# Moving pieces and turns ahead of the weighing in the slots that begin a new block of columns

## What is computed

```
x = x + layernorm(attention(layernorm(x)))
x = x + layernorm(ffn(layernorm(x)))

scores  = q k^T, causal mask, / sqrt(512)
weights = softmax(scores)
attention = (weights v) @ Wo
ffn = relu(h + coef * sin(theta + 0.1 h)) @ W2 + b2,   h = x @ W1 + b1
```

## Time and profile before

| | |
|---|---|
| median of 3 runs | 3336.05 us (3333.89 to 3338.84) |
| the profiled execution | 3334.82 us, its span 3332.8 us |
| busy: TensorE, VectorE, ScalarE, GpSimd | 3150.9, 2327.5, 2063.6, 1280.2 us |
| share of the span | 95%, 70%, 62%, 38% |
| mean granted clock of TensorE | 0.991 |
| attention, roughly | 587 to 1932 us of the span |

### The profile page before, as it was taken

How to read it: one execution, slowest core, us unless ns; L and a number is a source line. 1 busy time by engine, 2 the same in 40 slices (tenths; PEclk the granted TensorE clock), 3 DMA queues, 4 the chain that set the end, 5 groups by cost and what they waited for, 6 DMA issues and landing times. The chain is left out here.

```text
span 3332.8 us, 77773 instructions
## 1 busy us (share of the span) xinstructions
PE 3150.9 (95%) x30020; PEld 1830.6 (55%) x30020; DVE 2327.5 (70%) x4793; ACT 2063.6 (62%) x2451; POOL 1280.2 (38%) x574
## 2 busy tenths in 40 slices
PE   6999998899998999999999879999999999999998
PEld 3444444676766676667676634444444444444443
DVE  5665555688887888888888666666666666666665
ACT  2323332998988898989898935555555555555553
POOL 1000000898989898989898910000000000000000
PEclk9999999999999999999999989999999999999999
DMA  4564753123222222222222230000000000000000
GB/s 140 190 206 139 259 189 112 53 60 85 73 85 74 77 79 78 77 75 78 79 75 81 89 127 6 21 26 26 25 25 25 25 25 25 25 25 25 26 26 26
DMA packets 194113, 246.65 MB, mean 74 GB/s; under 512 B 16960, under 2 KB 135936, under 8 KB 191616
## 3 DMA queue, kind: packets, MB, share of 16 engines
q1 hardware_dynamic: 193792, 242.25, 23.2%
HBM read 148.87 MB, written 92.80 MB: 73 GB/s over the span
## 5 line engine op out<-in xcount | busy, mean ns | idle before, releaser
L1426 POOL TENSOR_TENSOR a_prob_lo<-a_prob,a_prob_hi 128x2048 f16<-128x2048 f32 (+2 forms) x448 | 1191.7, 2694 | 148.9 <-ACT a_prob_hi L1285 147.8
L313 DVE TENSOR_REDUCE u_mx<-a_pw 128x4 f32<-128x512 f32 (+1 forms) x1178 | 728.4, 656 | 192.2 <-PE a_pw L299 127.5
L1275 ACT ACTIVATE a_prob<-a_pst,a_lift,w_exp_scale 128x1024 f32<-128x1024 f32 (+1 forms) x640 | 707.4, 1123 | 131.7 <-PE a_pst L1212 90.7
L1285 ACT ACTIVATE a_prob_hi<-a_prob 128x2048 f16<-128x2048 f32 (+2 forms) x448 | 584.0, 1304 | 0.0
L1731 ACT ACTIVATE f_hidden_work<-f_ph,w_turn,w_fold 128x512 f32<-128x512 f32 x256 | 199.4, 779 | 586.5 <-PE f_ph L1777 586.0
L1777 PE MATMUL f_ph<-f_xT,f_w 128*128 128x512 f16 x2304 | 528.6, 379 | 0.0
L1798 PE MATMUL f_py<-f_w,f_act 128*128 128x512 f16 x2280 | 523.1, 379 | 0.1
L1212 PE MATMUL a_pst<-u_qp,u_kp 98*128 98x256 f16 (+1 forms) x2560 | 464.3, 263 | 36.8 <-ACT a_prob L1275 16.6
L228 POOL TENSOR_TENSOR s_ve<-s_mv,s_eps 128x4 f32<-128x4 f32 x31 | 8.9, 286 | 1273.0 <-DVE s_mv L214 1273.0
L1239 PEld LDWEIGHTS a_acc<-u_vt,a_prob_hi 128*128 128x128 f16 x9216 | 422.6, 96 | 128.7 <-POOL a_prob_lo L1426 38.2
L1239 PE MATMUL a_acc<-u_vt,a_prob_hi 128*128 128x33 f16 x9216 | 448.6, 178 | 43.2 <-POOL a_prob_lo L1426 34.4
(11 more groups left out here) (187 smaller groups left out, 4089.4 us busy)
## 6 DMA issues: line engine op xcount, KB each, us to landing
qk_parts<-q_stage SPq DMA_DIRECT2D x128, 256.0 KB, 3.3
u_qp<-qk_parts SPq DMA_DIRECT2D x192, 128.0 KB, 2.6
u_kp<-qk_parts SPq DMA_DIRECT2D x192, 128.0 KB, 2.7
v_parts<-q_vstage SPq DMA_DIRECT2D x16, 1056.0 KB, 5.3
u_vt<-v_parts SPq DMA_DIRECT2D x32, 528.0 KB, 4.3
q_x<-in_L_attn_h_dram SPq DMA_DIRECT2D x16, 1024.0 KB, 10.2
q_raw<-in_L_ffn_W_dram SPq DMA_DIRECT2D x16, 1024.0 KB, 8.1
u_xr<-in_L_attn_h_dram SPq DMA_DIRECT2D x64, 256.0 KB, 3.0
```

The source lines that it names most:

```text
L313: dve.tensor_reduce(out, src[:, 0:n * len(heads)].rearrange("p (h n) -> p h n", n=n), AX_X, ALU.max).then_inc(units.released, 1)
L1275: act.activation(prob[:, k % PR, :, off:QC], pst[:, k % 2, :, off:QC], ACT.Exp, scale=exp_scale, bias=lift[:, :]).then_inc(exp_done, 1)
L1285: act.activation(prob_hi[:, first % HR:first % HR + steps, :, off:QC], prob[:, first % PR:first % PR + steps, :, off:QC], ACT.Copy).then_i ...
L1426: pool.tensor_tensor(prob_lo[:, first % HR:first % HR + steps, :, off:QC], prob[:, first % PR:first % PR + steps, :, off:QC], prob_hi[:, f ...
```

## The change

In a slot where the weighed step has j = 0, what stood behind half 0 and half 1 of the weighing (items 2 and on) now stands behind the second part of the scores, in front of half 0. In all other slots the cuts (0, 1, 2, 3, all) give the order as before. No item is added or removed, and no other engine's program is touched.

```diff
@@ -1251,13 +1251,15 @@
                         e = stage.earlier(u, k, LAG)
                         items = stage.at(u, k)
 
+                        fresh = e is not None and STEPS[e[1]][1] == 0
+                        cuts = (0, 1, len(items), len(items), len(items)) if fresh else (0, 1, 2, 3, len(items))
 
                         for part in range(PARTS):
                             if part < 2 and stage.this:
                                 scores(i, u, k, range(part * HPG // 2, (part + 1) * HPG // 2))
                             if part >= 2 and e:
                                 weigh(i, *e, part - 2)
-                            for at, what, unit, m in (items[part:part + 1] if part < PARTS - 1 else items[part:]):
+                            for at, what, unit, m in items[cuts[part]:cuts[part + 1]]:
                                 shared(i, at, before, what, unit, m, stage)
```

## The result

| | before | after |
|---|---|---|
| median of the runs | 3335.56 us (4 runs) | 3357.61 us (3354.44 to 3361.07, 4 runs) |
| ratio, with its 95% interval | | 1.0065 (1.0053 to 1.0078) |
| the profiled execution | 3334.82 us, span 3332.8 | 3361.07 us, span 3359.1 |
| mean granted clock | 0.991 | 0.983 |
| length of units 0, 1, 2, 3 of a middle batch, where the clock stays full | 41.18, 45.15, 39.01, 42.2 us | 41.34, 45.54, 39.32, 42.8 us |

The kernel became slower by 22 us, 0.65%, more than the range reached (3338 to 3355). The last row of the table is the length of a unit, from its first score matmul to the next unit's, every matmul of the trace being counted into its slot in program order.

The account below looks back on a forecast made before the run. All four compute engines of attention have little room, so delays travel round their ring; six middle batches 8.5, the last 0.8 and batch 0 1.2 sum to 10.5 us, giving 3346 us, range 3338 to 3355.

Parts of the forecast that it names:

- The delay: Slots 8 and 12 of attention: moved items keep VectorE's pace, weighing follows, later slots start late; 1.41 us per middle batch.
- Batch 0: Slot 12 there: ScalarE nearly the bound, 0.3 us taken for each of four units, low end 0.05; slot 8 adds 0.
- The clock: TensorE's granted clock in attention: gaps of 0.3 to 0.6 us left it full, so the skill's warning was not borne out.
- rival E: Longer TensorE idles drop the clock once in each of 31 units, at most 1.65 us each, up to 51 us; chance 0.02.
- B: Delay absorbed by the waits of slots 10, 13 and 14: 0 to +6.7 us, about 3339; chance 0.30.
- C: Nothing absorbed, VectorE late as well in most units: +15 to +27 us, 3351 to 3363; chance 0.11.
- D: Faster: pieces fill a wait of the weighing in slot 8 (and 12), up to 8.1 us, 3328; chance 0.04.
- F: Moved items sit in slots where TensorE is not on the chain, so time stays at 3336; chance 0.01.
- A: The main forecast for the whole kernel: delay partly absorbed, +7 to +15 us; chance 0.52.

Follow-up runs that it names:

- Slot 12 alone: The new order applied only in slot 12, all other slots as in the kernel before: 3352.52 us, 1.0058 of the kernel before.
- slot 8 alone: The new order applied only in slot 8, all other slots as in the kernel before: 3340.88 against 3333.65 us, ratio 1.0021.
- piece 2 alone in front: Kernel before, but in slot 12 piece 2 stands ahead of both weighing halves, the turn behind them: 3341.61 us, 1.0021.
- the turn alone: Kernel before, but in slot 12 the turn of the maxima stands ahead of half 1, piece 2 between the halves: 3336.71 us, 1.0008.
- The extra matmuls: Changed kernel plus nine useless 248-column matmuls per unit in the waits of slots 8 and 12: 3350.50 us, 1.0052 of the kernel before.
- one piece less just in front of it: Kernel before with one piece moved from slot 12 to slot 17: 3318.69 against 3334.65 us, ratio 0.9951.

## Why the prediction was wrong

**The delay was right, in place and nearly in size.** The waits stayed where I put them: piece 2 at VectorE's pace, the weighing behind the turn, and a delay through exponentials 13 and 14 to slot 18. By unit I had said 0.09, 0.39, 0.28 and 0.65 us; measured 0.16, 0.39, 0.31 and 0.60. Batch 0: 0.3 said, 0.28 measured. The sum of undisturbed units over the kernel is 6 x 1.46 + 0.8 + 1.1 = 10.7 us, said 10.5.

That the numbers agree so well is in part luck. Slot 12 alone lengthened unit 1 by 0.4, not 0.35, since slot 13 begins 0.68 later and not 0.61 (between the turn and what follows it lie 0.18 us now, and 0.11 before); slot 8 alone gave unit 1 nothing, and not 0.04. In unit 0 slot 12 gave 0.05 where I had put 0. And the 0.60 of unit 3 is batch 1. In the others it grew by 0.3 to 1.3 us: slots 8 and 12 give 0.30 and 0.40 in batches 2 and 6, and of the 1.1 to 1.3 in batches 3 to 5 slots 5 to 8 have 0.8 to 0.9, for there the store of the maxima landed at 5.9 to 6.0 us after slot 3 began, against 5.3 to 5.5 before.

**The step that failed is "The clock".** I wrote that gaps of 0.3 to 0.6 us had left the clock full, and that the trace did not bear out what the Trainium skill says; rival E got a chance of 0.02. Thus the sum had no term for the clock. Yet the change makes longer gaps than any that the argument looked at. In unit 2 of batch 2, slot 12, half 0 waited for `a_o` and then piece 2 for the bank; after the change these are one wait, and the turn waits too (before, then after):

```profile
1019.19 0.22 PE L1239 MATMUL a_acc<-u_vt,a_prob_hi 128*128 128x33 f16 x2 [0.18 <-DVE a_o L1316]
...
1020.16 0.39 PE L294 MATMUL a_pw<-u_kp,u_qp 96*128 96x512 f16 x1 [0.50 <-DVE u_mx L313]
```

```profile
1026.79 0.39 PE L294 MATMUL a_pw<-u_kp,u_qp 96*128 96x512 f16 x1 [1.15 <-DVE u_mx L313]
1027.38 0.28 PE L305 MATMUL a_pw<-u_ident,u_mx 128*16 128x128 f32 x1 [0.21 <-DVE u_mx L313]
```

All fourteen units 0 and 2 of batches 1 to 7 have these idles within 0.1 us, and ten lost their clock. Slot 12 of units 1 and 3 idles 0.77 and 0.21 us, and none did. The longest idle alone does not tell: the run with piece 2 alone in front has the same 1.15 without the 0.21, and the one with the turn alone 0.50, 0.21 and 0.18, and each had two drops in the fourteen.

The Trainium skill (TensorE: Matmul & The Clock Gate, "A second HAM failure mode: psum-queue depth-cycling") tells of a kernel that cycles through PSUM banks and whose clock swings because TensorE idles briefly between groups of matmuls, frequently enough. After the change this trace agrees in kind, with ten grants of 0.50 behind waits for a bank, but what changed in slot 12 of these units is the length of the idles, two as before, and not how often they come.

Taking attention as a whole, from its first scores to the start of its last slot, it grew by 25.1 us in the profiled execution. Of these 10.7 are delay and some 12 the eleven drops, at 0.9 to 1.4 us each; the other 2 stand mostly in the units 3 above. That a drop costs less than E's 1.65 was within its bound; that there would be eleven in 31 units and not one in each was not foreseen. The profiled execution is the slowest of the four, with a granted clock of 0.983, where the others have 0.986 or 0.987 and took 2.5 to 6.6 us less, so these probably have fewer drops.

The extra matmuls show the cause: with the delay kept and the waits filled, the clock came back in every one of these slots, and units 0 and 2 had the length of the delay alone, save for the late store. Within the trace of the changed kernel the same holds: unit 2 of batch 5, with the same waits and no drop, took 39.32 us, and those with a drop 40.2 to 41.1.

**Rivals.** B fell: the first 0.26 us of a delay is absorbed and no more, as the turn alone shows. C fell: slots 8 and 12 of unit 3 kept 0.7 us by delay and not 0.9, and no other unit as much; that the time is in C's range is a coincidence. D fell: nothing got faster in slot 8. F fell. A and E were both true at once, and I had priced them as alternatives; their sum, 10.5 plus ten times 1.2, is 22.5 us, and 22 were measured. The count of ten is from the profiled execution, which is 3.5 us above the median, so this agreement too is rough.

What stays open: why the same slot with the same waits sometimes keeps its clock (batch 5, unit 2). The runs show only that drops turn up in other slots when the order or the filling of one slot is changed: slot 8 of unit 1 idles 0.81 and 0.55 us in the changed kernel and had none, and the same slot had two when slot 8 alone was changed.

## What to carry to other kernels

An item that waits for another engine should not be moved ahead of independent work that fills its wait: the wait keeps its end, and the filling comes on top. When waits of TensorE are merged or lengthened, expect a loss of clock behind them on top of the delay, and look at the granted clock slot by slot; neither the old gaps nor the longest new one told here where it would fall. And look for the chain that sets the period: here one piece less just in front of it gave 16 us, where none of the other orders tried gave any.

## What the runs showed of the hardware that was not expected

The granted clock fell to 0.50 for 3.4 us after stretches such as 1.84 us of work in 3.2, in ten of fourteen like slots, at 0.9 to 1.4 us each. Extra matmuls inside waits brought it back. But the added code is not free: with 6 per unit in the kernel before, which do nothing and end in time, it was slower by 13 us, and a 4 KB store landed 0.8 to 1.8 us late in slots where nothing had been added. In every such unit 0 or 2 a 16 KB packet of the instruction queue had begun just before, which points to the fetch as the cause and does not prove it.
